# A two-layer graph network on one core: a second engine fetches part of the gathered rows

## The chip, the cores and the metric

One core of a Trainium2 chip runs one program. The metric is device microseconds of that core, the median of the runs shown; less is better. The engines are named as in the profile: PE (TensorE), DVE (VectorE), ACT (ScalarE), POOL (GpSimd) and SP (SyncE). A quad is four tiles of 128 nodes, 512 nodes.

## What is computed

Two layers over a graph of 12500 nodes with 128 features and 212500 edges that are sorted by destination (every node also has an edge to itself). The first layer multiplies a source's row by a matrix that depends on the edge's relation, the second takes the mean of the neighbours; each adds its input and is normalised.

```python
W = jnp.einsum('rb,bio->rio', w_comp, weight)          # 16 relations out of 8 bases
h = jnp.einsum('ni,rio->rno', x, W)
msg = h[etypes, src]
node_repr = jax.ops.segment_sum(msg, dst, num_segments=N_NODES) + h_bias
x = _layernorm(x + node_repr, axis=-1)                 # x1

agg = jax.ops.segment_sum(x[src], dst, num_segments=n) # second layer, on x1
h_neigh = agg / deg[:, None] @ W_neigh
x = _layernorm(x + feat @ W_self + b_self + h_neigh, axis=-1)
```

## The kernel before

**Tiling.** Edges are cut into chunks of 128, one edge for each partition, and eight chunks make a group: 208 groups, of which the last has five chunks. The source rows of a chunk come with one indirect DMA, issued by POOL, whose indices are a column of `src_t`. PE multiplies them by one-hot columns that DVE makes (destination within a window of 21 nodes, times the relation's base factors), and DVE adds the windows to `acc`.

**First sweep** (the loop over `g`, one group in each turn). The first 24 groups (`PLAIN`) are narrow: they gather rows of x (512 bytes) from `x_in`, L1366. All others are wide: they gather rows of 1024 bytes from `table`, where each node's x stands beside its x1, L1370. Both layers' sums of such a group are made at once, as far as x1 is known: a quad's x1 is complete when its last edge has been summed, and is stored into `x1_rows` and `table` (L1273). Which quads are in is given by `front(g)`, with at least `BEHIND` = 6 groups between completion and use. A source beyond the front is marked early (`mark_early` adds `full_rows` to its index, so that it reads the half of `table` where zeros stand beside x), and the edge is summed again later for its x1 alone. Narrow groups have four times two slots in `rows` (eight), wide ones four slots; POOL waits before a group until PE has read the slot's last user (`rows_read`, `z_done`).

**Second sweep** (the loop over `j`, one late group in each turn). The 24 narrow groups are gathered once more, from `x1_rows`, then the late edges of the others, which DVE and PE pack meanwhile, unit by unit (twelve units of 8 or 16 groups, `pick`, `unpack`), into columns `idx_l`. `room[q]` columns are kept for a unit, worked out from `late_of(g)`. There are 116 late groups, and POOL gathers them at L1384, eight slots ahead at most. The last quads' products and normalisations run between them and end the kernel.

**Order on the other queues.** SP issues in the first sweep, turn by turn: the pieces of `table` (the first eleven turns), every four groups the edge types of the groups two blocks on (L1226, behind a wait for `eoh_ready`, which DVE gives for a block of four in the turn three groups before the block), and in the turns `out_at` the load of x of the quad after next and `store_x1` of the quad: rows into `x1_rows`, rows into `table` (for the first 20 quads), degrees into `deg_rows` (L1273, L1276, L1279). Between the sweeps POOL waits for the last two quads' stores. In the second sweep SP loads quads (L1254, L1263) and stores results (`store_out`, L1286). ACT copies each group's sums out of PSUM (L1423), and in the turns `staged_at` it stages a quad, takes the roots and normalises it (L1399).

**The setup** (until about 75 us) loads and transposes the indices, counts late edges and works out the thresholds `thr` by which edges are marked; if a flag says that the edges don't fit the assumptions, a general program runs instead, which is not in the trace.

## Time and profile before

| | us |
|---|---|
| median of 3 runs | 3921.51 |
| lowest, highest | 3912.53, 3926.23 |
| span of the profiled execution | 3299.5 |
| busy: POOL, PE, DVE, ACT | 2457.6, 2010.2, 1379.0, 317.5 |
| TensorE's granted clock, mean | 0.726 |

The span reaches from the first to the last instruction of the profiled execution; the runs' times are those of whole executions on the device, and the 622 us between the two are in no row of the trace. Register, branch, semaphore and DMA-issuing instructions are not counted as busy on SP and ACT; for POOL the writing of an indirect DMA's descriptors is. In the slices of the page, a digit is the busy share in tenths.

### The profile page before, as it was taken

How to read it: one execution, taken by the hardware profiler on the slowest of the kernel's cores; microseconds unless marked ns; L12 is line 12 of the kernel's file. 1: busy time of each engine (PE TensorE's matmuls, PEld its weight loads, DVE VectorE, ACT ScalarE, POOL GpSimd, SP SyncE). 2: the span in 40 equal slices, each digit the busy share in tenths (PEclk: the TensorE clock that was granted, in tenths of full speed). 3: DMA queues.
4: the chain of work that ended last, by engine and by line, in shares of the span. 5: the costliest groups of instructions: out<-in, count | busy, mean ns of one | idle time of the engine just before them, and what ended most of it. 6: DMA issues, size and time to landing. Idle time of an engine off the chain costs nothing.

```text
span 3299.5 us, 35621 instructions
## 1 busy us (share of the span) xinstructions
PE 2010.2 (61%) x12511; PEld 1948.2 (59%) x12511; DVE 1379.0 (42%) x3552; ACT 317.5 (10%) x572; POOL 2457.6 (74%) x2590
## 2 busy tenths in 40 slices
PE   1756677767766777767766777544454444445454
PEld 1756676767766777767766777544444444444444
DVE  5533333233323333333333333245656676666434
ACT  2110111011111111111111111100000000000001
POOL 7777777777777777777777777577777777777774
PEclk9877777777787777777777777655566666666666
DMA  2953444344444444444444443212222222222232
GB/s 76 306 159 106 126 123 122 109 122 122 124 122 121 122 121 121 120 122 122 124 122 120 118 118 110 84 53 63 62 62 63 63 72 63 72 63 72 74 94 68
DMA packets 256767, 346.87 MB, mean 105 GB/s; under 512 B 46902, under 2 KB 188735, under 8 KB 256584
## 3 DMA queue, kind: packets, MB, share of 16 engines
q0 software_dynamic: 106000, 265.39, 28.1%
q1 hardware_dynamic: 150584, 79.16, 8.2%
q8 instruction: 100, 1.64, 0.2%
q14 instruction: 83, 0.68, 0.1%
HBM read 313.37 MB, written 43.84 MB: 108 GB/s over the span
## 4 chain that ended last, share of the span: by engine, by line
POOL 68%; issue 22%; PE 4%; DMA 1%; DVE 1%; ACT 0%; POOLq 0%; DVEq 0%; SPq 0%; ACTq 0%
POOL rows L1370 38%; POOL rows L1384 26%; POOL rows L1366 4%; PE zps L1876 2%; DMA rows<-x_x_rows,src_t 1%; PE yps L1903 1%; PE yps L1888 1%; PE tps L1903 0%; PE zps L1998 0%; PE tps L1888 0%; DMA rows<-x_rows,picked_mem 0%; PE yps L1915 0%; ACT xout L1399 0%; DVE stats L1472 0%; DVE xout L1466 0%
## 5 line engine op out<-in xcount | busy, mean ns | idle before, releaser
L1370 POOL DMA_INDIRECT rows<-x_x_rows,src_t x1469 | 1393.1, 948 | 447.5 <-issue 443.3
L1876 PE MATMUL zps<-acc,rows 128*128 128x168 f32 x3322 | 792.9, 416 | 527.0 <-DMA rows<-x_x_rows,src_t 496.5
L1876 PEld LDWEIGHTS zps<-acc,rows 128*128 128x128 f32 x3322 | 737.4, 274 | 546.8 <-issue 527.4
L1384 POOL DMA_INDIRECT rows<-x_rows,picked_mem x725 | 690.3, 952 | 220.9 <-issue 220.6
L1998 PE MATMUL zps<-acc,rows 128*128 128x128 f32 x1450 | 305.6, 397 | 341.5 <-DMA rows<-x_rows,picked_mem 339.3
L1998 PEld LDWEIGHTS zps<-acc,rows 128*128 128x128 f32 x1450 | 287.1, 303 | 350.9 <-issue 326.8
L1584 DVE TENSOR_TENSOR acc<-acc,yps 128x63 f32 (+1 forms) x535 | 116.8, 218 | 770.7 <-PE yps L1903 685.7
L1562 DVE TENSOR_TENSOR acc<-oh,tps 128x1344 f32<-128x1344 f32 x208 | 323.2, 1554 | 142.1 <-PE tps L1867 119.3
L1423 ACT COPY acc<-zps 128x672 f32<-128x672 f32 x208 | 148.9, 717 | 1569.1 <-PE zps L1876 1569.1
L1584 DVE TENSOR_TENSOR acc<-acc,tps 128x63 f32 (+1 forms) x296 | 64.5, 218 | 423.5 <-PE tps L1903 379.0
L1384 POOL DMA_INDIRECT rows<-x_rows,src_t x192 | 182.0, 948 | 77.2 <-issue 58.2
L1888 PEld LDWEIGHTS yps<-oh,rows 128*128 128x128 f32 x1914 | 234.0, 196 | 0.0
L1888 PE MATMUL yps<-oh,rows 128*128 128x21 f32 x1914 | 227.6, 265 | 0.0
L1743 DVE TENSOR_TENSOR acc<-place_b,tps 128x1024 bf16<-128x1024 bf16 x184 | 222.7, 1210 | 0.0
L1366 POOL DMA_INDIRECT rows<-in_x_dram,src_t x144 | 138.3, 960 | 49.8 <-issue 49.8
L1903 PE MATMUL yps<-acc,picked_mem 128*128 128x168 f32 x1056 | 173.0, 318 | 0.0
L1903 PEld LDWEIGHTS yps<-acc,picked_mem 128*128 128x128 f32 x1056 | 169.8, 204 | 0.0
L1678 DVE TENSOR_TENSOR acc<-acc,zps 128x128 f32 (+1 forms) x461 | 121.3, 263 | 111.9 <-PE zps L1993 49.8
L1993 PE MATMUL zps<-oh,rows 128*128 128x21 f32 x384 | 82.9, 373 | 120.7 <-DMA rows<-x_rows,src_t 116.9
L1993 PEld LDWEIGHTS zps<-oh,rows 128*128 128x128 f32 x384 | 81.2, 321 | 123.3 <-issue 114.3
L1515 DVE TENSOR_TENSOR xin<-xin,tps 128x512 f32<-128x512 f32 x22 | 15.1, 687 | 324.5 <-PE tps L2012 324.5
L1967 PEld LDWEIGHTS yps<-acc 128*128 128x128 bf16 x1472 | 62.9, 108 | 121.2 <-DVE acc L1747 116.9
(257 smaller groups left out, 1886.8 us busy)
## 6 DMA issues: line engine op xcount, KB each, us to landing
rows<-x_x_rows,src_t POOLq DMA_INDIRECT x1469, 2.7
acc<-in_edge_type_dram SPq DMA_DIRECT2D x207, 64.0 KB
rows<-x_rows,picked_mem POOLq DMA_INDIRECT x725, 2.5
x_x_rows<-in_x_dram SPq DMA_DIRECT2D x20, 576.0 KB
x_x_rows<-zrow SPq DMA_DIRECT2D x20, 576.0 KB
xin<-in_x_dram SPq DMA_DIRECT2D x24, 256.0 KB, 3.3
x_rows<-xout SPq DMA_DIRECT2D x24, 256.0 KB
out_dram<-xout SPq DMA_DIRECT2D x24, 256.0 KB
```

What stands on the lines that cost most here:

```text
L1366: gather = pool.indirect_dma_start(out=rows[:, g % SLOTS, c, :], out_offset=None, in_=x_in, in_offset=bass.IndirectOffsetOnAxis(ap=src_t[: ...
L1370: gather = pool.indirect_dma_start(out=wide_rows[:, g % WIDE_SLOTS, c, :], out_offset=None, in_=table, in_offset=bass.IndirectOffsetOnAxis ...
L1384: pool.indirect_dma_start(out=rows[:, j % SLOTS, c, :], out_offset=None, in_=x1_rows[0:n_nodes, :], in_offset=bass.IndirectOffsetOnAxis(ap ...
L1423: nc.scalar.copy(zsb[:, g % 4].rearrange("p (h w) b n -> p h (w b n)", h=2), zduos[g % 2]).then_inc(w1.z_copied, 1)
L1562: nc.vector.tensor_tensor(a[:, g % 4], oh1[:, g % 6].unsqueeze(2).to_broadcast([P, CPG, n_bases, SPAN]), wcp[:, m % 2, g % HALF, :].rearra ...
L1584: add = nc.vector.tensor_tensor(target, target, windows_of(g)[:, first:3, c, :], ALU.add)
L1743: nc.vector.tensor_tensor(to_lane[:, t % UNROLL], place_b[:, 0, at].unsqueeze(2).to_broadcast([P, CPG, P]), lanes_p.unsqueeze(1).to_broadc ...
L1876: last = nc.tensor.matmul(zwins[g % 2][:, c // HALF, c % HALF // 2], slot_rows(g, c), a[:, g % 4, c], start=(c % 2 == 0), stop=(c % 2 == 1 ...
L1888: last = nc.tensor.matmul(windows_of(g)[:, 0, c // 2], wide_rows[:, g % WIDE_SLOTS, c, d:2 * d], oh1[:, g % 6, c], start=(c % 2 == 0), sto ...
L1903: last = nc.tensor.matmul(windows[p][:, 1], wb[:, b, :], two[:, :, b, :], start=(b == 0), stop=(b == n_bases - 1))
L1993: last = nc.tensor.matmul(sums_of(j, c // 2, SPAN), rows[:, j % SLOTS, c, :], oh1[:, j % 4, c], start=(c % 2 == 0), stop=(c % 2 == 1))
L1998: last = nc.tensor.matmul(sums_of(j, c0, P), rows[:, j % SLOTS, c, :], oh2[:, j % 4, c, :], start=(c == c0), stop=(c == c0 + n - 1))
```

## The change

- Two sets of groups are named. `hand_groups` are 23, 27, 31, 39, 43, 51, ... 199: every fourth group from 23 to 203, without every third after the first. `sp_lates` are the late groups 5, 11, ... 107. In them POOL gathers seven chunks. The eighth (`HAND_COL`) is fetched by SP with 128 DMAs of one row each, in four parts of 32 rows. A part first loads 32 byte offsets into registers with one call, then issues its DMAs (`fetch_rows`). Three buffers (`hand`, each 128 x 256 words) take turns. The lists for ACT (`act_hands`, `act_lates`) are empty.
- The parts are placed in SP's turns 8, 7, 5 and 4 groups ahead of the hand, or 6, 5, 3 and 2 ahead for the second of two hands four groups apart; in the second sweep 9, 8, 6 and 5 ahead, not before turn 0.
- The offsets of all groups' eighth chunks are made by DVE behind `mark_early` (`hand_f`), turned by PE at turn 14 and kept by ACT as `hand_i`; those of the late columns are turned by PE in `spread_base` and scaled by DVE in `unpack_last`.
- The x1 half of the eighth chunk of every fourth group is read by the front of 13 groups earlier (`HAND_LAG`, `hand_front`), in the marking, in the thresholds of the setup and in `late_of`.
- `store_x1` is issued by ACT behind the quad's normalisation; SP's load of x comes three turns later than before. Results (`store_out`) of all quads but the last three are issued by ACT; SP's second sweep runs by late groups.

```diff
+HAND_COL = CPG - 1
+HAND_BUFS = 3
+HAND_EVERY = 4
+HAND_LAG = 13
+SP_ROWS = 32
+ACT_ROWS = 16
...
+    def hand_front(g):
+        return 0 if g < PLAIN else min(FRONT, max(2 * (g - HAND_LAG) - 2 - 2 * BEHIND, 0) // 17)
...
     def late_of(g):
-        return P * CPG * (16.0 / 17.0 - early_share * QUAD * front(g))
+        lagging = front(g) - hand_front(g) if g % HAND_EVERY == HAND_EVERY - 1 else 0
+        return P * (CPG * (16.0 / 17.0 - early_share * QUAD * front(g)) + early_share * QUAD * lagging)
...
+            hand_groups = range(PLAIN - 1, last_group - 3, HAND_EVERY)
+            sp_hands = [g for i, g in enumerate(hand_groups) if i == 0 or i % 3]
+            hand_groups = sp_hands
+            act_hands = []
+            act_at, sp_at = {}, {}
+            for i, g in enumerate(sp_hands):
+                second = i and g - sp_hands[i - 1] == HAND_EVERY
+                for part, ahead in enumerate((-6, -5, -3, -2) if second else (-8, -7, -5, -4)):
+                    sp_at.setdefault(g + ahead, []).append((i, part))
...
+            def fetch_rows(engine, only, r0, many, indices, source, to, landed):
+
+                row = source.shape[1] * 4
+                to_bytes = to.bitcast(U8)
+                from_bytes = source.rearrange("n f -> (n f)").bitcast(U8)
+                _, starts = nc.values_load_multi_w_load_instructions(
+                    indices[0:1, r0:r0 + many], engines=only, min_val=0, max_val=(source.shape[0] - 1) * row,
+                    skip_runtime_bounds_check_because="the first byte of a source's row, in the half of the table for it")
+                for e in range(many):
+                    engine.dma_start(to_bytes[r0 + e:r0 + e + 1, :],
+                                     from_bytes[bass.ds(starts[e], row)].rearrange("(o f) -> o f", o=1)).then_inc(landed, 16)
+
+            def fetch_hand(engine, only, hands, i, part, many):
+
+                g = hands[i]
+                if part == 0:
+                    engine.wait_ge(hand_kept, 1)
+                    if i >= HAND_BUFS:
+                        before = hands[i - HAND_BUFS]
+                        if narrow(before):
+                            engine.wait_ge(w1.z_done, before + 1)
+                        else:
+                            engine.wait_ge(rows_read, before - PLAIN + 1)
+                    if not narrow(g):
+                        engine.wait_ge(table_in, table_parts)
+                    if hand_front(g):
+                        k = hand_front(g) - 1
+                        engine.wait_ge(stored1[k % 2], stores(k))
+                indices = hand_i[g % P:g % P + 1, g // P, :]
...
+            sp_lates = [j for j in range(5, late_groups - 4, 6) if HAND_COL in late_chunks(j)]
+            act_lates = []
...
+                for part, ahead in enumerate((-9, -8, -6, -5)):
+                    sp_late_at.setdefault(max(0, j + ahead), []).append((i, part))
...
-                        if g in out_at:
-                            if out_at[g] + 2 < all_quads:
-                                load(n1, out_at[g] + 2, x_in, False)
-                            if out_at[g] == 0:
-                                sp.wait_ge(table_in, table_parts)
-                            store_x1(out_at[g])
+                        if g - 3 in out_at and out_at[g - 3] + 2 < all_quads:
+                            load(n1, out_at[g - 3] + 2, x_in, False)
+                        for i, part in sp_at.get(g, ()):
+                            fetch_hand(sp, SP_ONLY, sp_hands, i, part, SP_ROWS)
...
-                        real = real_chunks(g)
-                        for c in range(real):
+                        pooled = pooled_chunks(g)
+                        for c in pooled:
...
                             normalise_quad(n1, staged_at[g])
+                            if staged_at[g] == 0:
+                                act.wait_ge(table_in, table_parts)
+                            store_x1(staged_at[g])
...
                         rows_arrived(w1, g)
                         for c in range(real_chunks(g)):
+                            if by_hand(g, c):
+                                _, landed, count = hand_place(g)
+                                pe.wait_ge(landed, count)
```

## Rows read from the trace of the kernel before

**Rows 1.** The page: span, engines, POOL's slices, DMA queues, chain

```profile
span 3299.5 us, 35621 instructions
...
PE 2010.2 (61%) x12511; PEld 1948.2 (59%) x12511; DVE 1379.0 (42%) x3552; ACT 317.5 (10%) x572; POOL 2457.6 (74%) x2590
...
POOL 7777777777777777777777777577777777777774
...
q0 software_dynamic: 106000, 265.39, 28.1%
q1 hardware_dynamic: 150584, 79.16, 8.2%
...
POOL 68%; issue 22%; PE 4%; DMA 1%; DVE 1%; ACT 0%; POOLq 0%; DVEq 0%; SPq 0%; ACTq 0%
POOL rows L1370 38%; POOL rows L1384 26%; POOL rows L1366 4%; PE zps L1876 2%; DMA rows<-x_x_rows,src_t 1%; PE yps L1903 1%; PE yps L1888 1%; PE tps L1903 0%; PE zps L1998 0%; PE tps L1888 0%; DMA rows<-x_rows,picked_mem 0%; PE yps L1915 0%; ACT xout L1399 0%; DVE stats L1472 0%; DVE xout L1466 0%
```

**Rows 2.** POOL's timeline from 1014 us: start us, us, instruction, idle before

```profile
1015.59 0.96 POOL L1370 DMA_INDIRECT rows<-x_x_rows,src_t  x1 [0.30 <-issue]
1016.85 0.95 POOL L1370 DMA_INDIRECT rows<-x_x_rows,src_t  x1 [0.30 <-issue]
```

**Rows 3.** L1370's and L1384's forms, L1370's group: duration min/median/max ns, starts

```profile
L1370 POOL DMA_INDIRECT rows<-x_x_rows,src_t x1469: 942/946/1146, 259.2 to 2098.6; - x184
...
L1384 POOL DMA_INDIRECT rows<-x_rows,picked_mem x725: 940/945/1452, 2359.1 to 3269.0; - x182
L1384 POOL DMA_INDIRECT rows<-x_rows,src_t x192: 940/945/1297, 2118.6 to 2357.8; - x192
...
L1370 POOL DMA_INDIRECT rows<-x_x_rows,src_t x1469 | 1393.1, 948 | 447.5 <-issue 443.3 <-PE yps L1888 3.0 <-PE tps L1888 1.2
```

**Rows 4.** Between the sweeps: SP's last store, POOL's next gather

```profile
2116.74 0.25 SPq L1279 DMA_DIRECT2D deg_rows<-acc  x1
...
2118.61 0.94 POOL L1384 DMA_INDIRECT rows<-x_rows,src_t  x1 [19.06 <-DMA deg_rows<-acc]
```

**Rows 5.** Waits: engine line, waited for, total us, times, longest

```profile
PE zps L1876 <- DMA rows<-x_x_rows,src_t: 496.5, 162, 6.9
```

**Rows 6.** Stretch: its us, busy PE, PEld, DVE, ACT, POOL; clock, DMA share

```profile
259.00:2098.00 1839.00, 1313.27 (x7870) 1294.06 (x7870) 579.59 (x1473) 204.94 (x352) 1391.90 (x1468) 0.78 0.41 120
...
2120.00:3280.00 1160.00, 554.55 (x3880) 521.56 (x3880) 662.95 (x1715) 54.90 (x130) 871.14 (x916) 0.62 0.25 68
```

**Rows 7.** SP's DMAs of one row, base's and deg_rows' forms

```profile
L414 SPq DMA_DIRECT2D base<-duo_bases x1: 221/221/221, 46.6 to 46.6; - x1
...
L1279 SPq DMA_DIRECT2D deg_rows<-acc x25: 249/412/536, 190.6 to 2116.7; - x25
```

**Rows 8.** SP's eight DMAs of L410 in a chain, as in group 7

```profile
L410 SPq DMA_DIRECT2D wc_blk<-in_L_gnn_w_comp_dram x8: 419/420/428, 9.6 to 12.8; - x8
```

**Rows 9.** Register loads: four values or one on DVE, one on SP

```profile
L1666 DVEq TENSOR_LOAD <-base_l x92: 318/343/675, 2374.8 to 3282.6; - x92
...
L697 SPq TENSOR_LOAD <-span x1: 465/465/465, 75.7 to 75.7; - x1
```

**Rows 10.** SP's edge types and stores into the table

```profile
L1226 SPq DMA_DIRECT2D acc<-in_edge_type_dram x207: 593/594/3270, 76.3 to 1967.2; - x104
...
L1273 SPq DMA_DIRECT2D x_x_rows<-xout x20: 508/509/523, 190.0 to 1772.1; - x20
```

**Rows 11.** SP's timeline at the start of the second sweep

```profile
2124.02 0.51 SPq L1263 DMA_DIRECT2D rdeg<-deg_rows  x1
```

**Rows 12.** Timeline of all engines around a quad's normalisation

```profile
1008.02 0.16 DVE L1485 SCALAR_TENSOR_TENSOR shift<-mv,rstd 128x4 f32<-128x4 f32 x1
...
1009.77 0.70 ACT L1423 COPY acc<-zps 128x672 f32<-128x672 f32 x1
...
1012.49 0.90 PE L1876 MATMUL zps<-acc,rows 128*128 128x168 f32 x2 [4.95 <-DMA rows<-x_x_rows,src_t]
```

**Rows 13.** POOL's narrow gathers as a group: busy us, mean ns

```profile
L1366 POOL DMA_INDIRECT rows<-in_x_dram,src_t x144 | 138.3, 960 | 49.8 <-issue 49.8
```

More of the change, by code:

```diff
@@ L217, in gnn_kernel @@
         zero = sb("zero", [P, 1])
+        hand = sb("hand", [P, HAND_BUFS, 2 * d])
+        hand_i = sb("hand_i", [P, 2, P], I32)
+        lag_i = sb("lag_i", [P, 1], I32)
+        lag = sb("lag", [P, 1])
         oh1 = sb("oh1", [P, 6, CPG, SPAN])
@@ new lines, in gnn_kernel, with by_hand, hand_place @@
+            for i, g in enumerate(act_hands):
+                free = [e for e in range(max(g - 16, hand_turn_at + 1), g - 2) if e not in staged_at and e not in cleared_at and e not in act_at]
+                assert len(free) >= P // ACT_ROWS, g
+                for part, e in enumerate(free[-(P // ACT_ROWS):]):
+                    act_at[e] = (i, part)
+            def by_hand(g, c):
+                return c == HAND_COL and g in hand_groups
+            def hand_place(g):
+                if g in act_hands:
+                    i = act_hands.index(g)
+                    return act_ring[:, i % HAND_BUFS], act_in1[i % HAND_BUFS], 16 * P * (i // HAND_BUFS + 1)
+                i = sp_hands.index(g)
+                return hand[:, i % HAND_BUFS], hand_in1[i % HAND_BUFS], 16 * P * (i // HAND_BUFS + 1)
@@ new lines, in fetch_hand @@
+            def fetch_hand(engine, only, hands, i, part, many):
[14 more added lines that the diff above has]
+                indices = hand_i[g % P:g % P + 1, g // P, :]
+                buf, landed, _ = hand_place(g)
+                if narrow(g):
+                    fetch_rows(engine, only, part * many, many, indices, x_in, buf[:, 0:d], landed)
+                else:
+                    fetch_rows(engine, only, part * many, many, indices, table, buf, landed)
@@ L1099, in products_before, with pooled_chunks @@
+            def pooled_chunks(g):
+                return [c for c in range(real_chunks(g)) if not by_hand(g, c)]
             def products_before(g):
@@ L1170, in steps_before @@
                 return min(j, PLAIN) * (DUOS - 1) + late_steps
+            places_for = [("start", e * 3 // 4) for e in range((final_group(0) + 3) * 4 // 3)]
+            for k in range(last_quad - 2):
+                places_for += [((k, "kept"), final_group(k) + 5)]
+                idle = max(1, (final_group(k + 1) - final_group(k) - 2) * 4 // 3)
+                places_for += [((k, "out"), final_group(k) + 6 + e * 3 // 4) for e in range(idle)]
+            act_late_at = {}
+            at = len(places_for)
+            for i, j in reversed(list(enumerate(act_lates))):
+                for part in reversed(range(P // ACT_ROWS)):
+                    at = max(e for e in range(at) if places_for[e][1] <= j - 2)
+                    act_late_at.setdefault(places_for[at][0], []).insert(0, (i, part))
             closing = range(last_quad - 2, all_quads)
@@ L1595, in mark_early @@
                             g0 = etiles + c0 // CPG
-                            after(dve, marked, 1 + 2 * part)
+                            after(dve, marked, 1 + 3 * part)
                             nc.vector.tensor_tensor(
@@ L1845, in bank_free @@
                             pe.wait_ge(s_loopc, holder[1] + 1)
+                        elif holder and holder[0] == "hand":
+                            pe.wait_ge(hand_kept, 1)
                         elif holder:
@@ L1861, in turn_loops, with turn_hands @@
                         last.then_inc(s_loops, 1)
+                    def turn_hands():
+                        bank_free("hand", 0)
+                        pe.wait_ge(hand_shown, 3)
+                        for h in range(2):
+                            last = nc.tensor.transpose(hand_rows[:, h, :], hand_f[:, h * P:(h + 1) * P], ident[:, :])
+                        last.then_inc(hand_turned, 1)
                     def scale_by_relation(m):
@@ L1997, in late_sums_of @@
                                 for c in range(c0, c0 + n):
-                                    last = nc.tensor.matmul(sums_of(j, c0, P), rows[:, j % SLOTS, c, :],
+                                    last = nc.tensor.matmul(sums_of(j, c0, P), late_rows(j, c),
                                                             oh2[:, j % 4, c, :], start=(c == c0),
```

172 lines of the change are left out of this document (143 added, 29 removed).

## The prediction

> **What bounds the kernel now.** The page comes first [rows 1]: POOL is busy 74% of the span, no other engine above 61%, and its digit in the 40 slices is 7 from the first to the last but one. A 7 in every slice, not a 9, could mean waiting, so the next view is the chain of waits: 68% of it is POOL and 22% "issue", its three largest lines being POOL's gathers. The timeline of POOL shows what the 7 is [rows 2]: a gather takes 0.94 to 0.96 us, then 0.30 us passes for which no other engine is named, then the next begins. So one gather of 128 rows costs a fixed pitch. From its first wide gather at 259.2 to its last at 2098.6 POOL issues 1469, (2098.6 - 259.2) / 1468 = 1.253 us each [rows 3]; in the second sweep (3269.0 - 2118.6) / 916 = 1.256 us [rows 3]. Outside that pitch POOL waited 3.0 and 1.2 us for PE in the first sweep [rows 3] and once 19.06 us between the sweeps [rows 4]. PE, in contrast, waits for gathers: 496.5 us in the first sweep alone, in 162 times [rows 5]. In the stretch of wide gathers PE is busy 1313 of 1839 us, DVE 580, ACT 205; in the second sweep 555, 663 and 55 of 1160 [rows 6]. A group of eight chunks lasts 10.0 us and PE has 7.1 us of work in it. The time is the number of POOL's gathers times 1.25 us.
>
> **What the change takes from POOL.** First sweep: hands are groups 23, 27, ... 203 (46), of which every third after the first is left out (15): 31 gathers go. Second sweep: late groups 5, 11, ... 107: 18 gathers go. But the eighth chunk of every fourth group is now judged against an x1 front 13 groups older, so more edges are left to the second sweep; working the rooms of the twelve units through the code, two units (88 for 87, 51 for 50) grow by one column each: 919 late chunks instead of 917 (the 725 + 192 of [rows 3]), two gathers more. Late groups stay 116. Net 31 + 18 - 2 = 47 gathers, and 47 x 1.253 = 58.9 us.
>
> **What SP gets, first sweep.** A hand is four parts of 32 rows. A part is one register load of 32 values and 32 DMAs of one row each. The trace has no DMA with its address in a register and no load of 32 values, so both are bounded. One-row DMAs of a plain address: from DRAM to SBUF 0.221 us (one case, 3.3 KB), to DRAM 0.249 to 0.536 us, median 0.412 [rows 7]. The stores to DRAM stand right behind one of 128 rows or nearly so (L1273, L1276); the new ones stand behind one row again, and their direction is that of the 0.221 case. So I take 0.221, keep 0.257 (the short stores, 0.249, with a little over) as the bound of my own case and 0.412 as the rival's. Eight DMAs in a chain start (12.8 - 9.6) / 7 = 0.457 us apart at 0.420 each [rows 8], a gap of 0.04 us; 0.043 is taken. A register load of four values takes DVE 343 ns and of one value (the last late group) 318 ns [rows 9], so (343 - 318) / 3 = 8.3 ns a register; SP's own load of one value took 465 ns [rows 9]. Then 32 values: 0.465 + 31 x 0.0083 = 0.72 us, or 0.0225 us a row. Sum: 0.221 + 0.043 + 0.0225 = 0.287 us a row (0.323 with the bound), 9.2 us (10.3) a part.
>
> Does it fit? In the stretch of [rows 3] lie 30 hands, 3840 rows. The stretch will last 1839.4 - 30 x 1.253 = 1802 us; of that SP spends 184 x (0.594 + 0.043) = 117 us on edge types and some 10 us on loads of x [rows 10], the loads at a price of 0.4. That leaves 1675 / 3840 = 0.436 us a row against 0.287. SP is 69% used. The worst run of parts is three within four groups, 28 to 31 us of about 39. SP also starts early: its wait at the head of four groups is for the relations of those four, which DVE makes in its turn three groups before, so parts placed 8 to 2 groups ahead begin some 3 groups sooner still, and a hand whose last part is placed 2 groups ahead has about 4 groups, 39 us, of cover. Queued behind the parts on SP are the edge types (needed by DVE a block later) and the x loads, moved 3 groups later with 17 groups to use them in. The stores, whose gates stood between SP's loads, leave its queue.
>
> **Second sweep.** 18 hands are 2304 rows in 3269.0 - 2118.6 - 16 x 1.256 = 1130 us, less some 21 us for loads: 0.481 us a row are to be had. The tight one is late group 5, whose four parts all stand at the start: SP is free at 2124.5 [rows 11], 128 x 0.287 = 37 us later it is 2161; POOL ends the seven other chunks at 2118.6 + 47 x 1.25 = 2177. Cover 16 us, gone at 0.41 us a row; even then PE alone waits, for POOL has eight slots.
>
> **The transfers.** Hardware queue 1 moves 150584 packets in 8.2% of 16 engines, 29 ns each of 0.53 KB; POOL's queue 140 ns each of 2.5 KB [rows 1]. If all 3840 packets of rows of the first sweep fell on one DMA engine at the higher price, that is 0.54 ms of its 1.80 ms on top of the 0.41 share that it has [rows 6]: 0.71. Priced at nothing on the path: a gather's landing (2.7 us) follows each group anyway.
>
> **What ACT gets.** Per quad three issues, at most 0.509 + 0.509 + 0.412 us and the gaps, 1.5 us [rows 7, 10], 25 times, then 22 stores of results. Behind them is the copy of the next sums (L1423): at 1009.77 it ran right behind the normalisation, and the next sums of PE began at 1012.49 [rows 12]; their group needs only the copy before that one. Hidden; uncovered it would cost 25 x 1.5 = 38 us of PE time, still inside the 526 us that PE has over in [rows 6]. No DMA from ACT is in the trace; only the last two quads' stores, ahead of the end of POOL's 19.06 us wait, are on the path, where the last costs SP 0.25 us [rows 4]: I take 0, bounds -1 (the hop to SP goes) and +2 us.
>
> **The rest at nothing.** DVE's extra steps in the setup, the marking and unpacking are some forty small ones (0.16 us for one on 4 columns [rows 12]; doubled for the wider, 13 us) beside 1.2 ms of its idle time; PE gets 14 transposes; SP's wait for the turned lists at its turn 15 holds it until about group 14, and the relations behind it are wanted from group 17 on. The front lag asks for stores that are complete a group and more before SP comes to them.
>
> **Sum.** Span 3299.5 - 58.9 = 3240.6 us. Around the profiled span lie, against the median of the runs, 3921.5 - 3299.5 = 622.0 us that the trace doesn't show; kept as they are: 3240.6 + 622.0 = 3862.6 us.
>
> **Rivals.**
> A, forecast, 3863: chance 0.75. Its own range: if timed runs stretch everything evenly (3921.5 / 3299.5 = 1.19), the gain is 70 and the time 3852; the runs themselves spread by 9 us to the lower side: 3843.
> B, SP becomes the bound, ending slower: a row costs the median of the one-row stores, 0.412 + 0.043 + 0.0225 = 0.48 us. PE then waits for every hand in the first sweep, POOL for PE's slots (four wide ones), and it lasts 3840 x (0.48 - 0.436) = 169 us longer: 4031. It bounds from 0.436 us a row and makes the kernel slower from 0.436 + 58.9 / 3840 = 0.451 us. For it: a register address and the load may cost more than shown. Against it: the clean one-row cases lie at 0.22 to 0.26. Chance 0.12, of it 0.02 between these two points, within 0.3% of no change.
> C, register loads are paid one by one: each register at the 318 ns of a load of one gives 0.221 + 0.043 + 0.318 = 0.582 us a row, +561 us in the first sweep and 2304 x (0.582 - 0.481) = +233 in the second: about 4657. It decides from 0.187 us a register. Against it the 8.3 ns of [rows 9]. Chance 0.03.
> By "Runtime: NRT & Kernel Launch" of the Trainium skill (section Instruction fetch mechanics) a register load costs about 200 ns per register even in bulk; by that figure, an estimate from this page, a row would cost 0.46 us and the kernel would end near 3970, slower. By that rule four registers would cost 800 ns; [rows 9] disagree with 343, though with another engine and source.
> D, POOL's own gathers stretch while SP's rows pour in: in the narrow groups, the first of which run beside the laying of the table, a gather's mean was 960 instead of 948 ns [rows 3, 13]. 12 ns on 2530 gathers: 30 us, 3893. Chance 0.06.
> E, what lies around the span grows with the program: 622 us over 35621 instructions is 17.5 ns each, and 49 x 132 = 6470 more on SP would cost 113 us: 3976. Nothing in the trace speaks for it but that the 622 us are unexplained. Chance 0.04.
>
> **Numbers.** The range takes A and D with the spread of the runs: 3843 to 3900, 0.81. A measurement of this kernel can tell about 0.3% from no change. Faster by more: A and D, 0.81. Within: 0.02. Slower: the rest of B, C and E, 0.17.
>
> **What would show it.** Right: POOL's gathers 2578 - 47 = 2531 at the same 1.25 us, hand groups with seven gathers in 8.8 us, SP's row DMAs at 0.22 to 0.26 us, the span near 3241. Wrong: PE's waits before L1876 name a DMA from SP, POOL waits for PE before wide gathers (B, C); the register load of 32 values far over 0.7 us (C); gathers at 960 ns (D); span right, time not (E).

## The result and the profile after

The changed kernel took 4690.61 us (median of 4 runs, 4680.43 to 4693.62) against 3921.68 us of the kernel before beside it: a ratio of 1.195, 95% interval 1.193 to 1.1975. It is slower by 19.5%, where 1.5% faster was forecast.

The same kernel before takes about 3298 us in some sessions on a chip (called undisturbed below) and 3892 to 3938 us in others (disturbed), so a run is compared only with the kernel before in its own session; the profile shown ahead of the prediction is of the first kind, the times beside it are of the second.

The changed kernel's page (span; engines; POOL's slices; queues; chain by engine and by line), from a disturbed session:

```profile
span 4689.8 us, 48462 instructions
...
PE 2182.0 (47%) x12529; PEld 2052.1 (44%) x12529; DVE 1388.4 (30%) x3585; ACT 319.8 (7%) x573; POOL 2403.8 (51%) x2543
...
POOL 6644545545544644644644644545455554554442
...
q0 software_dynamic: 104016, 260.34, 19.4%
q1 hardware_dynamic: 127988, 66.90, 4.9%
q10 hardware_dynamic: 35140, 17.46, 1.3%
...
SPq 58%; issue 34%; PE 3%; DVE 1%; another core or an unknown queue 1%; ACT 0%; DMA 0%; DVEq 0%; ACTq 0%
SPq L1185 47%; SPq L1181 8%; SPq L1401 2%; PE zps L2106 1%; PE yps L2132 0%; SPq L1429 0%; PE yps L2118 0%; PE tps L2132 0%; DVE acc L1890 0%; ACT xout L1563 0%; DVE acc L1762 0%; SPq L1438 0%; PE tps L2094 0%; DVE stats L1672 0%
```

Against [rows 1]: POOL has 47 instructions less (2590 to 2543), just the gathers that were to go, but it is busy 51% of the span instead of 74%. The chain that ended last (the last instruction, followed back from wait to wait) was 68% POOL; now 58% is SP's queue, nearly all of it the row DMAs (L1185) and the register loads (L1181). The span equals the run's time within 2 us, so here nothing lies around it.

The same kernel's gathers in the two sweeps, SP's rows and SP's register loads (duration min/median/max ns, first and last start):

```profile
L1532 POOL DMA_INDIRECT rows<-x_x_rows,src_t x1439: 940/946/1098, 311.4 to 2945.6; - x180
...
L1548 POOL DMA_INDIRECT rows<-x_rows,picked_mem x713: 938/944/1271, 3294.1 to 4626.5; - x179
L1548 POOL DMA_INDIRECT rows<-x_rows,src_t x188: 938/944/1112, 2981.3 to 3289.9; - x188
```

```profile
L1185 SPq MOVE hand<-x_x_rows x3840: 1/29/1396, 359.8 to 2889.9; - x192
L1185 SPq DMA_DIRECT2D hand<-x_x_rows x3840: 2/225/1398, 359.9 to 2889.9; - x192
L1185 SPq MOVE hand<-x_rows x2304: 1/29/1409, 2989.5 to 4617.2; - x192
L1185 SPq DMA_DIRECT2D hand<-x_rows x2304: 1/228/1437, 2989.6 to 4618.3; - x192
```

```profile
L1181 SPq TENSOR_LOAD <-hand_i x140: 3/2124/2501, 263.9 to 3387.6; - x140
```

A gather still takes 946 ns as in [rows 3]. But the stretch of wide gathers lasts 2945.6 - 311.4 = 2634 us and the second sweep 4626.5 - 2981.3 = 1645. SP's rows run from end to end of both: 2530 us for the first sweep's 120 parts of 32 rows and 1629 for the second's 72. From a part's register load to its last DMA pass 19.9 us on average in the first sweep and 22.2 in the second. 120 x 19.9 = 2390 of the 2533 us between the first such load and the last row, and in the other 143 SP issues the edge types and loads of x; in the second sweep 72 x 22.2 = 1601 of 1631. SP's queue is full from end to end.

What PE and POOL wait for (engine line, waited for, total us, times, longest):

```profile
PE zps L2106 <- DMA hand<-x_x_rows: 512.6, 20, 40.0
...
POOL rows L1532 <- PE yps L2118: 424.5, 36, 30.5
...
PE zps L2233 <- DMA hand<-x_rows: 340.6, 14, 36.4
...
POOL rows L1548 <- PE zps L2233: 328.1, 26, 30.4
```

PE waits for SP's rows, up to 40 us at a time, and POOL for the buffers that PE then doesn't free. In [rows 3] POOL waited 3.0 and 1.2 us for PE in the first sweep, and in the kernel before of a disturbed session (e11_before) 62.4 and 42.0.

The kernel before in a disturbed session (span; chain; group of the wide gathers; group of a matmul at L1888; the stretch of wide gathers, with its us, the busy us of PE, PEld, DVE, ACT and POOL, the granted clock, the DMA share and GB/s) and then the span and the same matmul group in an undisturbed one:

```profile
span 3906.2 us, 35621 instructions
...
another core or an unknown queue 36%; PE 23%; issue 18%; DVE 17%; DVEq 3%; ACT 1%; DMA 0%; SPq 0%; ACTq 0%
...
L1370 POOL DMA_INDIRECT rows<-x_x_rows,src_t x1469 | 1393.9, 949 | 808.6 <-issue 414.1
...
L1888 PE MATMUL yps<-oh,rows 128*128 128x21 f32 x1914 | 288.7, 285 | 180.6 <-issue 180.1
...
313.00:2484.00 2171.00, 1437.59 (x7864) 1366.24 (x7862) 580.23 (x1473) 207.00 (x354) 1393.00 (x1469) 0.71 0.35 102
```

```profile
span 3298.5 us, 35621 instructions
...
L1888 PE MATMUL yps<-oh,rows 128*128 128x21 f32 x1914 | 229.4, 266 | 0.0
```

These lines are the warning that the trace of before could not give. In the disturbed session POOL is idle 808.6 us ahead of its wide gathers instead of 447.5 [rows 3], and it isn't on the chain (36% of which has no owner in this view); PE, which undisturbed goes through L1888 without one pause, stops there for 180 us with nothing to wait for. PE has become the limit of this stretch: of its 2171 us PE is busy 1438, another 557 pass on PE without a wait, and no wait for a gather is left, where undisturbed PE waited 496.5 us for them [rows 5]. Its busy time grew too, from 1318 to 1438 us for the same groups, at a mean granted clock of 0.71 instead of 0.77 (e1_before); whether the pauses lower the clock isn't shown. From its first wide gather to its last the kernel before takes 2170.6 us there (313.3 to 2483.9) and 1331.0 in the second sweep. The change adds 2634.2 - 2170.6 = 463.6 and 1645.2 - 1331.0 = 314.2, together 778 of the 784 us between the two spans.

### The profile page after: what moved, and what is told of

Read it like the earlier page. It is cut to its first block, busy times and chain, and to the rows that moved or that the text cites. A ratio compares the mean times of both kernels' runs of the same rounds, so it can differ in the third digit from the quotient of the medians.

```text
span 4689.8 us, 48462 instructions
## 1 busy us (share of the span) xinstructions
PE 2182.0 (47%) x12529; PEld 2052.1 (44%) x12529; DVE 1388.4 (30%) x3585; ACT 319.8 (7%) x573; POOL 2403.8 (51%) x2543
## 4 chain that ended last, share of the span: by engine, by line
SPq 58%; issue 34%; PE 3%; DVE 1%; another core or an unknown queue 1%; ACT 0%; DMA 0%; DVEq 0%; ACTq 0%
SPq L1185 47%; SPq L1181 8%; SPq L1401 2%; PE zps L2106 1%; PE yps L2132 0%; SPq L1429 0%; PE yps L2118 0%; PE tps L2132 0%; DVE acc L1890 0%; ACT xout L1563 0%; DVE acc L1762 0%; SPq L1438 0%; PE tps L2094 0%; DVE stats L1672 0%
## 5 line engine op out<-in xcount | busy, mean ns | idle before, releaser
L1532 POOL DMA_INDIRECT rows<-x_x_rows,src_t x1439 | 1362.6, 947 | 1302.4 <-PE yps L2118 424.5
L1548 POOL DMA_INDIRECT rows<-x_rows,picked_mem x713 | 674.3, 946 | 662.5 <-PE zps L2233 328.1
L2106 PEld LDWEIGHTS zps<-acc,rows 128*128 128x128 f32 x3260 | 702.1, 265 | 199.6 <-issue 198.5
L2233 PE MATMUL zps<-acc,rows 128*128 128x128 f32 x1426 | 275.9, 353 | 426.8 <-DMA hand<-x_rows 340.6
L2233 PEld LDWEIGHTS zps<-acc,rows 128*128 128x128 f32 x1426 | 246.5, 259 | 442.5 <-issue 442.1
L2118 PEld LDWEIGHTS yps<-oh,rows 128*128 128x128 f32 x1858 | 307.9, 245 | 205.6 <-issue 205.6
L2118 PE MATMUL yps<-oh,rows 128*128 128x21 f32 x1858 | 296.1, 298 | 198.1 <-issue 198.0
L2106 PE MATMUL zps<-acc,hand 128*128 128x168 f32 x62 | 26.1, 520 | 520.6 <-DMA hand<-x_x_rows 512.6
L2106 PEld LDWEIGHTS zps<-acc,hand 128*128 128x128 f32 x62 | 14.9, 293 | 529.5 <-DMA hand<-x_x_rows 521.3
L2198 PE MATMUL yps<-acc 128*128 128x24 bf16 (+8 forms) x1472 | 78.8, 193 | 298.6 <-issue 218.6
L2118 PEld LDWEIGHTS tps<-oh,rows 128*128 128x128 f32 x1020 | 170.2, 250 | 76.2 <-issue 75.9
```

What stands on the lines that cost most here:

```text
L1532: gather = pool.indirect_dma_start(out=wide_rows[:, g % WIDE_SLOTS, c, :], out_offset=None, in_=table, in_offset=bass.IndirectOffsetOnAxis ...
L1548: pool.indirect_dma_start(out=rows[:, j % SLOTS, c, :], out_offset=None, in_=x1_rows[0:n_nodes, :], in_offset=bass.IndirectOffsetOnAxis(ap ...
L2106: last = nc.tensor.matmul(zwins[g % 2][:, c // HALF, c % HALF // 2], slot_rows(g, c), a[:, g % 4, c], start=(c % 2 == 0), stop=(c % 2 == 1 ...
L2118: last = nc.tensor.matmul(windows_of(g)[:, 0, c // 2], slot_x1(g, c), oh1[:, g % 6, c], start=(c % 2 == 0), stop=(c % 2 == 1 or c == real_ ...
L2233: last = nc.tensor.matmul(sums_of(j, c0, P), late_rows(j, c), oh2[:, j % 4, c, :], start=(c == c0), stop=(c == c0 + n - 1))
```

## The experiments

Times are medians in us; "before" is the kernel before in the same session. Edits are against the changed kernel unless said otherwise.

### Is it the change, and which part? (undisturbed)

> The kernel before, unchanged, to see in a new trace what its median of 3922 us is made of, since the profiled execution at hand had a span of 3299.5 us. Theory 1 (the whole execution is stretched): POOL's gathers follow each other at 1.5 us and not 1.25 us, span about 3920. Theory 2 (622 us lie outside): the gathers stand at 1.25 us and the span is about 3300.

Measured: 3300.16 (before 3298.03). The profile's span was 3298.5. The 622 us that lay "around the span" are gone: they never lay around it, they are the difference between the two kinds of session.

```diff
+            sp_hands = []
             hand_groups = sp_hands
...
-            sp_lates = [j for j in range(5, late_groups - 4, 6) if HAND_COL in late_chunks(j)]
+            sp_lates = []
```

> The changed kernel with both lists of hands empty: SP fetches no row, POOL gathers all chunks (two more than before, for the older front), stores are with ACT, lists and marking stay. If the rows that SP fetches are the whole loss, this ends within 10 us of before. If the stores on ACT, the lists or the older front cost something, it ends slower by that.

Measured: 3298.47 (before 3298.03). Everything but the rows, the stores on ACT and the longer setup included, costs nothing.

```diff
-                _, starts = nc.values_load_multi_w_load_instructions(...)
+                starts = [(source.shape[0] // 2 + (r0 + e) * 48) * row for e in range(many)]
...
-                                     from_bytes[bass.ds(starts[e], row)]...
+                                     from_bytes[starts[e]:starts[e] + row]...
```

> SP's row DMAs with addresses known at build time: no register loads and no moves; the rows fetched are wrong ones (that part of the sums is not computed). Theory R (registers are the cost): with 2.1 us of load for each part and 0.03 us of move for each row gone, and nothing else wrong, parts fall from 20.8 to about 9 us and the time under before. Theory G (a row DMA is held up while gathers move their packets): rows still take 0.6 us in the mean beside gathers, only loads and moves go, 3840 + 2304 rows by 0.1 us: time about 4000 to 4200 us, still slower than before.

Measured: 3239.6 (before 3298.03), 58.4 us less. The forecast for 47 gathers was 58.9.

```diff
-                    engine.dma_start(to_bytes[r0 + e:r0 + e + 1, :],
+                    engine.dma_start(to_bytes[r0 + e:r0 + e + 1, :].rearrange("p (k f) -> p k f", k=16),
```

(the source is cut the same way)

> Each row is fetched as 16 pieces of 64 (32) bytes instead of one piece, so that it falls on 16 DMA engines instead of one. Theory G1 (all rows queue on one DMA engine behind the gathers' packets there): the stalls of 0.7 us go, a row costs its issue of 0.42 us, a part about 17 us, the time falls to about 4200. Theory G2 (the descriptors themselves, or the queue to all engines, are held up): the stalls stay and with 16 times the packets the time rises over 4700.

Measured: 3255.16 (before 3298.03). A miss as an experiment: the packets in the trace had the same sizes and numbers as without the edit, so it is the changed kernel once more and tells nothing of spread rows.

> The changed kernel itself. The runs behind the result had before at 3922 us and the change at 4691, while on the chip of the first experiments before takes 3298 us, as its first trace does, and SP's clean parts take 12.7 us. Theory S (the loss belongs to executions in which instructions and DMAs of the whole core are stretched, and SP's row chain suffers most): beside a before of about 3298 us the change takes about 3255 us, faster by 1.3%; beside a before of about 3922 it is slower by 20% again. Theory C (the change is slow by itself): slower by 20% beside either.

Measured: 3257.14 (3254.88 to 3260.86, before 3297.86), ratio 0.9875, interval 0.9859 to 0.9892. The same program that is 19.5% slower in one session is 1.25% faster in another. Its chain, the rows and loads, and two of its waits:

```profile
span 3259.1 us, 48462 instructions
...
POOL 61%; issue 21%; SPq 7%; PE 5%; DMA 1%; DVE 1%; ACT 0%; ACTq 0%; DVEq 0%; POOLq 0%
```

```profile
L1185 SPq MOVE hand<-x_x_rows x3840: 29/29/39, 269.4 to 1975.7; - x192
L1185 SPq DMA_DIRECT2D hand<-x_x_rows x3840: 224/225/759, 269.5 to 1975.8; - x192
```

```profile
L1181 SPq TENSOR_LOAD <-hand_i x140: 2027/2177/3547, 209.2 to 2300.9; - x140
```

```profile
PEld zps L2106 <- DMA hand<-x_x_rows: 74.6, 5, 24.6
PE zps L2106 <- DMA hand<-x_x_rows: 73.3, 5, 24.3
```

The medians are those of the result's profile: 225 ns a DMA, 29 ns the MOVE ahead of it, 2.1 to 2.2 us a load of 32 values. What differs is the spread of their records (2 to 1398 ns a DMA there) and the time between their starts. The timeline of SP in two comparable places (start, us, instruction), undisturbed and disturbed:

```profile
1110.08 17.65 SPq L1185 DMA_DIRECT2D hand<-x_x_rows  x48
```

```profile
1126.39 23.50 SPq L1185 DMA_DIRECT2D hand<-x_x_rows  x32
```

48 rows in 17.65 us with a 2.2 us load among them are 0.32 us each; 32 rows in 23.50 us are 0.73.

> The kernel before once more, for its trace on the same chip as the run above. If before takes 3298 us: the same trace as before. If it takes 3922: theory S says that POOL's gathers or their landings are longer by 19% in the trace, or that waits of 0.7 us stand between SP's and POOL's instructions.

Measured: 3296.12 (before 3297.86).

First hands alone and late hands alone are each one of the two edits of e2_no_hands:

> Hands in the first sweep alone; the second sweep's eighth chunks are all POOL's. Against before: 31 gathers less, 2 more, 29 x 1.253 = 36 us faster where the core is undisturbed; by theory C and in a disturbed execution most of the loss (3840 of 6272 rows and the POOL waits of 645 us before wide gathers) stays: 450 to 550 us slower.

Measured: 3279.34 (before 3297.86), 18.5 us less. Its 31 gathers less the two added are 29, worth 36.3: half is lost.

> Hands in the second sweep alone. Against before: 18 gathers less, 2 more, 16 x 1.25 = 20 us faster where the core is undisturbed; in a disturbed execution the rest of the loss, 200 to 300 us slower.

Measured: 3277.02 (before 3297.86), 20.8 us less, of 20.1 expected from 16 gathers net. So the undisturbed loss lies in the first sweep alone. PE's five waits in e5_after, 73.3 us, end between 322.7 and 711.9 us and shrink from 24.3 to 2.8: a backlog that is worked off. The first part starts at 209.2 us, when ACT has just copied the turned lists, and twelve parts of 12.7 us are due at once.

### What is late in a disturbed session?

```diff
             def by_hand(g, c):
-                return c == HAND_COL and g in hand_groups
+                return False
...
+                        engine.wait_ge(hand_in1[i % HAND_BUFS], 16 * P * (i // HAND_BUFS))
...
             def late_by_hand(j, c):
-                return c == HAND_COL and j in late_hands
+                return False
```

(PE's wait for a late hand goes as well, and SP has the same kind of wait ahead of the second sweep's buffers.)

> SP fetches all 49 hands' rows with the same loads, moves and DMAs, but nobody waits for them or reads them: POOL gathers every chunk again (SP itself waits until a buffer's last rows have landed). It separates what the row chain does to others from what waiting for it costs. Beside a before of 3298 us: if the rows' packets and instructions cost POOL and PE nothing, 3298 + 2.5 us for the two more gathers; if they slow the gathers (12 ns each), 3330. Beside a before of 3922 us, by the theory that only the wait for late rows makes the change slow there: about 3922; by the theory that SP's 12700 instructions themselves hold up PE's: clearly more, over 4000.

Measured: 4750.6 (before 3933.4). POOL gathers all chunks, no row of SP's is waited for by PE (only SP waits, before it uses a buffer again), and the time stays. Its chain is 57% SP's queue, and its waits:

```profile
DVE acc L1755 <- DMA acc<-in_edge_type_dram: 840.6, 42, 38.7
...
PE tps L2253 <- DMA rdeg<-deg_rows: 495.3, 16, 50.3
```

Whatever is queued on SP behind the rows comes late: the edge types for DVE, the degrees for PE. It is SP's queue that has become the bound, not the hand-over of rows. By the number alone the second theory above (SP's instructions hold up PE's) would have come true, but PE's own pauses did not grow: 849 us here, 1006 in the kernel before (table below).

```diff
-            sp_hands = [g for i, g in enumerate(hand_groups) if i == 0 or i % 3]
+            sp_hands = [g for i, g in enumerate(hand_groups) if i > 3 and i % 3]
```

> The first four places of the list (groups 23, 27, 31, 35) have no hand, so SP begins with group 39 instead of 23: three hands less. In the trace of the change beside 3298 us PE waited 73 us for rows of the first hands and POOL 19 us for PE behind that, since SP is free for hands only from 209 us on and a part takes 12.7 us. Theory (backlog at the start): those 19 us come back less 3 x 1.25 us of gathers: about 3242 us. Rival (the rows are late throughout): 3257 + 3.8 = 3261 us. Beside 3922 us the waits stand in all groups and little changes.

Measured: 4605.14 (before 3933.4). The backlog at the start isn't the cause here: with 46 of 49 hands the loss stays.

> The kernel before, for its trace beside a before of 3922 us. On that chip the traces of the changed kernel show halts of some 0.7 us between back-to-back instructions of SP (2536 of 12518) and of PE (742 of 11512), most of them while gathers move packets, and on the others none. Theory (the halts are the chip's, and before pays them on PE alone): some 700 to 1000 halts of PE, PE busy or halted all the time and POOL waiting for PE by about 600 us in sum, gathers still 0.95 us. Rival (before's 620 us come from something else): few halts on PE, longer gathers or landings. On a chip of 3298 us: the known trace.

Measured: 3907.86 (before 3905.76), span 3906.2: also a disturbed run has nothing around its span. Its lines stand above.

```diff
-            sp_hands = [g for i, g in enumerate(hand_groups) if i == 0 or i % 3]
+            sp_hands = [g for i, g in enumerate(hand_groups) if i % 3 == 1]
...
-            sp_lates = [j for j in range(5, late_groups - 4, 6) if HAND_COL in late_chunks(j)]
+            sp_lates = [j for j in range(5, late_groups - 4, 12) if HAND_COL in late_chunks(j)]
```

> One hand in twelve groups instead of two, and every second of the late hands: 15 + 9 hands, 22 gathers less in all. Beside a before of 3298 us: 22 x 1.253 = 27.6 us faster, 3270. Beside 3922 us, theory (SP is the bound there, about 83 us for a hand of four parts of 20.8 us): a hand in 12 groups fits into the about 140 us that 12 groups take there, so SP stops being the bound: about 3900 us. Rival (SP's chain slows PE and POOL whatever its share): halfway between, about 4300 us.

Measured: 3962.66 (before 3905.76). With half the rows SP has 2% of the chain, and 57 us are left of the 769 by which the medians of the result lay apart; yet they are 57 us more than before, although POOL has 22 gathers less. Part of them is again SP's: the second sweep's gathers last 1362.1 us instead of 1331.0, and in it PE waits once, until 2703.7 us, for the first late hand. Its four parts all stand at the start, and the first two took 67.5 and 48.1 us there.

```profile
PE zps L2228 <- DMA hand<-x_rows: 49.8, 1, 49.8
```

The rows without register loads, the edit of e3_static:

> SP's row DMAs with addresses known at build time (wrong rows fetched), beside a before of about 3910 us if this chip is of that kind. There a back-to-back instruction of SP is halted for some 0.7 us in about 37 of 100 cases while gathers move packets, in 4 of 100 otherwise. Theory (halts go by instruction): without the move a row has one instruction instead of two, so its pitch falls from 0.60 to 0.27 + 0.14 = 0.41 us, a part to 13 us, SP is no bound any more and the time falls from 4691 to before's 3910 or a little under. Rival (halts go by DMA or by row): the pitch falls by the move's 0.09 us alone, to 0.51 us, parts take 16 us and the time stays over 4100. Beside 3298 us: 3240 again.

Measured: 3960.91 (before 3938.35). SP issues as many rows as in the changed kernel, with one instruction for each instead of two and no register loads, and is no bound any more: its queue has 1% of the chain, and the time is some 730 us below the changed kernel's. Undisturbed and disturbed:

```profile
L1183 SPq DMA_DIRECT2D hand<-x_x_rows x3840: 211/245/1245, 253.4 to 1952.8; - x192
```

```profile
L1183 SPq DMA_DIRECT2D hand<-x_x_rows x3840: 2/243/1408, 321.0 to 2428.6; - x192
```

Its mean pitch is 0.299 us undisturbed and 0.459 disturbed, against 0.330 and 0.595 of the changed kernel. One instruction less a row saves 0.03 us undisturbed and 0.14 disturbed; the rival in the expectation (the pitch falls by the MOVE's own time) had 0.51 us and a time over 4100.

> No hands, the stores on ACT, beside a before of about 3910 us if this chip is of that kind. Theory: the stores, lists and marking cost nothing there either, within 10 us of before. Rival: ACT's DMAs or the loads moved three groups later cost where PE is late already, 30 to 60 us more, which would explain the 54 us by which one hand in twelve was slower. Beside 3298 us: the same again.

Measured: 3917.8 (before 3938.35), no cost of the rest of the change when disturbed either.

```diff
-                out=wide_rows[:, g % WIDE_SLOTS, c, :], out_offset=None, in_=table,
+                out=wide_rows[:, g % WIDE_SLOTS, c, 0:d], out_offset=None,
+                in_=table.rearrange('n (h f) -> (n h) f', h=2),
```

(against the kernel before)

> The kernel before, whose wide gathers fetch rows of 512 bytes instead of 1024 (the x1 halves of the slots keep old data and the rows are wrong ones: the first sweep's sums are not computed). As many gathers, descriptors and instructions, half the bytes. Beside a before of about 3910 us, theory (the halts of PE follow the bytes that gathers move): the halts in the first sweep fall to about half and the time by 250 us or so. Rival (they follow the gathers as such): the same time as before. Beside 3298 us: the same, 3298.

Measured: 3913.75 (before 3938.35). POOL's queue on its page:

```profile
q0 software_dynamic: 82496, 169.12, 16.8%
```

It moved 169 MB instead of 265, and PE's pauses stayed (856 against 869, next table). They don't follow the bytes of the gathers.

> The version without the first three hands once more, timed, since its first run stood beside a before of 3933 us and gave 4605. Beside a before of 3298 us: 3242 us, ratio 0.983, faster than the change's 0.9875; if the late rows of the first hands are not what costs the change 16 us against 47 x 1.253, then 3261 us. Beside 3930: 4600 again.

Measured: 4552.1 (4543 to 4566, before 3898.25), ratio 1.1679, interval 1.1643 to 1.1716.

> As the run before: 3242 us beside a before of 3298, by the rival 3261; beside 3900 again some 4570.

Measured: 3248.11 (before 3302.32), ratio 0.9833, interval 0.9804 to 0.9861: undisturbed, and with 44 gathers less it gains 54.2 of 44 x 1.253 = 55.1 us. It is the fastest that I have for such a session among the kernels that fetch the right rows. Its chain:

```profile
POOL 67%; issue 22%; PE 5%; DMA 2%; DVE 1%; ACT 0%; DVEq 0%; SPq 0%; ACTq 0%; POOLq 0%
```

> One hand in twelve groups, to stand beside its disturbed run of 3963 us. Beside a before of 3298 us: 22 gathers less, 27.6 us, 3270 us. SP is used at half, so no wait for late rows is expected beyond the first hand. Beside 3900 us: 3950 again, SP no bound and the gathers that are saved worth nothing, since PE is late there by its own halts.

Measured: 3277.57 (before 3302.32), ratio 0.9922: 24.7 us of 27.6.

### What the disturbed sessions have

Two things were counted from the starts and ends in the traces. On PE: weight loads that begin over 0.4 us after the end of the one before and wait for no semaphore. On SP: of two neighbouring row instructions (MOVE or DMA), how often the second starts over 0.6 us after the start of the first, parted by how many packets of gathers began in the same microsecond, at least 16 or at most 4.

```
                      PE: pauses, their us   SP: late starts     >=16      <=4
before, undisturbed        0
change, e5_after           1                    8 of 12348      0.1%     1.5%
static, e3_static          0                   23 of 6177       0.4%     0.0%
before, e11_before       869   1006
change, the result       747    865          2389 of 12348     35.7%     3.8%
e9_unused                720    849          2526 of 12348     35.7%     4.0%
e10_late_start           793    899          2348 of 11592     36.2%     4.0%
e16_late_start           788    867          2301 of 11592     35.0%     3.3%
e12_one_in_12            867   1018          1832 of 6048      40.8%     8.7%
e13_static               852   1048          2004 of 6177      39.7%    12.9%
e14_no_hands             831    956
e15_half_bytes           856    974
```

On SP a late start is mostly 0.7 us after the one before, some are 1.4 and a few 2.1; PE's weight loads show the same steps. In a disturbed session 35 to 41 of 100 of SP's row instructions come late while gathers move, whether a row costs two instructions or one and whether anyone waits for it. The time they take fits roughly: 2389 x 0.7 = 1.67 ms over 6272 rows is 0.27 us, and the mean pitch within a part rose from 0.330 to 0.595. On PE they make 1006 us in the kernel before, more than the 608 by which its spans differ (3906.2 - 3298.5), of which 558 lie in the stretch of wide gathers; the rest must have lain beside other waits. POOL has none: of some 2250 gathers and other instructions in e11_before that wait for nothing, not one starts over 0.4 us after the end of the one before. The packets themselves are alike in both kinds (a gather's median 182 to 184 ns, a row's 44 to 46), and so is POOL's gather (means of 947 to 951 ns).

One thing in the records themselves speaks for caution. In the result's trace 1964 of the 12348 row instructions start less than 25 ns after the one before, and 1492 of 6272 row DMAs are recorded with under 100 ns; in e5_after no start is closer than 57 ns and no DMA shorter than 224. So after a pause the instructions stand bunched, and a single pause can in part be a late record. The time is real none the less: spans and times agree within 4 us.

## Why the prediction failed, step by step

**622 us around the span, kept as they are.** The first step that failed. A span of 3299.5 beside times of 3912 to 3926 was kept as an offset; e1_before and e11_before show spans of 3298.5 and 3906.2 for 3300.16 and 3907.86 us, so nothing is around it. The trace showed another session than the times. The gap of 19% said that some 600 us were in none of my rows, and all my slack was read from these rows. The sign would have told that the rows are of another kind of session than the times; it would not have told what SP does in it.

**POOL bounds the kernel.** True of the trace, and of undisturbed runs. In the disturbed before POOL isn't on the chain and PE waits for no gather in the first sweep, so gathers saved were worth about nothing there: half the hands (e12) gave +57 us where 22 gathers less would be -28.

**47 gathers at 1.253 us.** Right as a term: e3_static measured 58.4 for 58.9, the late part 20.8 for 20.1, e17 54.2 for 55.1.

**What a row costs SP.** This is the step that the direction failed on. 0.287 us was forecast, with 0.323 as the bound, against 0.436 to be had; in the result's run a row took 19.9 / 32 = 0.62 us in the first sweep (mean, register load included). Undisturbed the medians give 0.322 + 2.18 / 32 = 0.390. The DMA was right (225 ns for 221), and what was missing is the MOVE of 29 ns ahead of each, which no row of before showed; the load of 32 values was 2.18 us (median of e5_after) and not 0.72. Extrapolating from the difference between one and four values on DVE [rows 9] by 8.3 ns a register was the mis-sized term: it is 68 ns. That still fits the budget: 0.390 is 89% of 0.436, where 0.287 is 66% (the 69% of the prediction is a slip). From 89% to over 100% it took the disturbed session: there the median DMA is the same 225 ns, but the mean pitch is 0.595 us instead of 0.330. The prediction's sign of being right, row DMAs at 0.22 to 0.26 us, was met even so, since a median doesn't show the pauses.
The rule of the Trainium skill ("Runtime: NRT & Kernel Launch", section Instruction fetch mechanics), some 200 ns for each register even in bulk, is three times too much here, as my 8.3 ns was eight times too little; by the measured 68 ns neither rival C nor its lighter form arises.

**SP's wait for the turned lists, at nothing.** I had the wait (until about group 14) and priced it at nothing. At 12.7 us a part, not 9.2, the twelve parts of the first three hands take 152 us from 209.2, and the first hands come late: most of the 18 us that are missing from the gain (58.9 - 40.7), and e17 gets them back but for 1 us by beginning with group 39.

**The second sweep fits**, with late group 5's cover gone at 0.41 us a row: right at 0.390, undisturbed. Disturbed it is gone, as the 49.8 us of e12 show.

**Transfers and ACT at nothing:** right. Wide gathers kept their mean, 949 ns in e5_after for 948 (so rival D is out, and its +30 us), and e2_no_hands has +0.4 us with ACT's stores in place.

**Between the sweeps, -1 to +2 us.** Too narrow for one profile. The wait of [rows 4], 19.06 us there and 21.0 in e1_before, is 20.4 in e2, e3, e17 and e18, so unchanged; but it is 25.6 in e5_after, the slowest of its four runs, and no run shows why. In the result's run it is 34.75, which is the session's more than the change's: from the last wide gather to the first late one pass 35.7 us there and 2518.2 - 2483.9 = 34.3 in e11_before.

```profile
2981.29 0.94 POOL L1548 DMA_INDIRECT rows<-x_rows,src_t  x1 [34.75 <-DMA deg_rows<-acc]
```

**The rivals.** B was the mechanism that took place: SP the bound, PE waiting for hands and POOL for PE's slots, and beyond that the edge types behind them (e9). Its price, 0.48 us a row from the median of the one-row stores, was too low, and so was its loss, 169 us. A disturbed first sweep has 2170.6 us for 3840 rows, or 0.53 each once some 143 us for edge types and loads are off; the rows took 0.62, and 2390 + 143 = 2533 us are 362 more than there is. The sweep became 464 us longer; the other 101 lie ahead of SP's first wide part and behind its last row, when the stretch of wide gathers runs without SP's rows (46 and 56 us). C's 4657 is near the 4691 by luck: its 0.318 us a register is 0.068 in truth. E would have the growth outside the span; it is all inside. Its 6470 further instructions were 12841, since each row has a MOVE as well.

So the direction failed on the price of a row on SP, which put SP at two thirds of its time when it was full, and the range with it: its bounds came from rows of a session without pauses. In such a session the change brought -40.7 us for the -58.9 forecast, the right sign with too much by 18.

**Still open.** What the pauses are. They show on PE and SP between instructions with nothing to wait for, and on SP mostly while gathers move; that the gathers make them is a correlation, as is that it is not their bytes (e15 left the number of gathers as it was). A run with no gathers in flight was not tried. Nor is it known why a session has them: chip number 0 was seen with and without. Every run here was recorded with its span, so a part of the recording in them can't be excluded. Of the 57 us of e12 some 26 (all that lies outside the second sweep) have no cause that I could show. The 23 of e13, one run against one, are near the spread: e14_no_hands lies 20.6 below the same kernel before.

## What to carry to other kernels

Put the profiled span beside the timed runs before anything else: where they are apart by 19%, the trace is of another state of the machine than the times, and its slack must not be spent. A queue that is 89% full by medians has no room for pauses of 0.7 us, and taking instructions out of it brought it back within bounds (e13); 128 row-wise DMAs with a MOVE each in place of one gather turn 1.25 us of POOL into 51 us of SP undisturbed and 83 disturbed. Start such a helper only where its inputs have been ready for as long as its backlog needs (group 39 instead of 23: 14 us won undisturbed), and carry a change through both kinds of session before it is called faster.

## What was not expected of the hardware

- A kernel on one core has two levels, stable within a session, 3298 and about 3892 to 3938 us, with pauses of 0.7 us and multiples between instructions of PE and SP in the second (869 on PE, 1006 us in all, against none), none on POOL, while POOL's gathers and the packets keep their durations.
- A DMA whose address is in a register costs SP 225 ns and a MOVE of 29 ns, with gaps 0.322 us; with a fixed address 0.294 us. A register load of 32 values takes 2.18 us on SP (median, undisturbed), 68 ns each.
- 3840 rows of 1 KB and 2304 of 0.5 KB through the same DMA engines as the gathers lengthened no gather: a mean of 949 ns with them (e5_after) and 948 without (e1_before).
